# Pairs of (batch, expert) sorted by expert on the chip: 24 of 32 expert units run two batches at a time from stationary weights staged by DMA, 8 one by one

## The reference, cut to what matters

```python
x = x + (einsum('btc,oc->bto', x, W_base) + b_base + 2.0 * lora(x, cond_8))   # first layer
def mlp(x, gate, up, down):                    # 128 -> 512 -> 128
    return (gelu(x @ gate) * (x @ up)) @ down
w, sel = top_k(softmax(cond_8), 2);  w = w / w.sum()
out = sum over the 2 selected experts e of each batch b:  w[b, e] * mlp(x[b], gate[e], up[e], down[e])
out = x + out + mlp(x, shared_gate, shared_up, shared_down)
```

## Time and profile before

| | us |
|---|---|
| median of 3 runs | 146.32 (146.22 to 146.63) |
| the profiled execution: span from first to last instruction | 144.9 |
| TensorE busy | 138.4 |
| VectorE busy | 77.0 |
| ScalarE busy | 73.5 |
| GpSimd busy | 29.7 |
| first product of the shared phase starts | 16.3 |
| first product of the expert phase starts | 52.8 |

### The profile page before, as it was taken

The page is one execution under the profiler, slowest core; times in us unless marked ns, Lnnn a source line. Parts: engine busy times, 40 slices in busy tenths (PEclk is TensorE's granted clock), DMA queues, the critical chain, the costliest instruction groups (busy, mean ns, idle before and its releaser), DMA issues.

```text
span 144.9 us, 3121 instructions
## 1 busy us (share of the span) xinstructions
PE 138.4 (96%) x807; PEld 116.2 (80%) x808; DVE 77.0 (53%) x129; ACT 73.5 (51%) x129; POOL 29.7 (21%) x39
## 2 busy tenths in 40 slices
PE   7899999999899899999999999999999999999991
PEld 6567876767678678889889889889889889889891
DVE  2799899998997986233233233233233233233220
ACT  3235979659759564544344344344344344344340
POOL 2027799831332211011011011011011011010000
PEclk9999999999999999999999999999999999999999
DMA  3997867991000000000000000000000000000001
GB/s 67 286 342 266 295 226 243 264 291 29 0 0 0 0 0 0 5 18 0 18 18 0 18 18 0 18 18 1 18 17 1 18 17 2 18 16 2 18 15 26
DMA packets 10101, 9.44 MB, mean 65 GB/s; under 512 B 1904, under 2 KB 6768, under 8 KB 10096
## 3 DMA queue, kind: packets, MB, share of 16 engines
q1 hardware_dynamic: 9776, 9.31, 21.3%
q10 hardware_dynamic: 320, 0.07, 0.2%
HBM read 8.32 MB, written 1.05 MB: 65 GB/s over the span
## 4 chain that ended last, share of the span: by engine, by line
PE 83%; DVE 5%; ACT 5%; DMA 2%; issue 2%; SPq 0%; DVEq 0%
PE bank L684 20%; PE bank L666 10%; PE bank L668 10%; PE bank L667 10%; PE bank L675 10%; PE bank L623 3%; PE bank L609 3%; PE bank L607 3%; PE bank L608 3%; PE bank L560 3%; DMA xn<-in_x_dram 2%; PE bank L624 2%; PE bank L625 2%; DVE hT_lo L472 2%; PE bank L554 2%
## 5 line engine op out<-in xcount | busy, mean ns | idle before, releaser
L464 DVE SCALAR_TENSOR_TENSOR work<-bank,wgt,work 128x512 f32<-128x512 f32 x32 | 24.0, 751 | 48.1 <-PE bank L668 26.0
L281 ACT ACTIVATE work<-bank 128x512 f32<-128x512 f32 x48 | 28.7, 598 | 39.6 <-PE bank L668 32.0
L684 PE MATMUL bank<-wexd,hT 128*128 x256 | 33.8, 275 | 0.0
L684 PEld LDWEIGHTS bank<-wexd,hT 128*128 128x128 f32 x256 | 31.1, 192 | 0.0
L666 PE MATMUL bank<-wex,xst 128*128 x64 | 27.8, 434 | 0.0
L295 ACT COPY hT<-bank 128x512 f32<-128x512 f32 x32 | 18.8, 586 | 16.6 <-PE bank L675 16.6
L668 PE MATMUL bank<-wex,xst 128*128 x64 | 25.1, 393 | 0.0
L667 PE MATMUL bank<-wex,xst 128*128 x64 | 25.0, 391 | 0.0
L223 POOL CAST xst<-x1s 128x256 fp32r (+1 forms) x16 | 7.3, 462 | 71.1 <-PE bank L668 71.0
L675 PE MATMUL bank<-ident,work 128*128 128x128 f32 x128 | 19.1, 272 | 0.0
L675 PEld LDWEIGHTS bank<-ident,work 128*128 128x128 f32 x128 | 15.8, 139 | 4.1
(11 more groups left out here) (80 smaller groups left out, 135.1 us busy)
## 6 DMA issues: line engine op xcount, KB each, us to landing
raw_ex<-n_L_cond_skill_gate_dram SPq DMA_DIRECT2D x8, 256.0 KB, 3.1
raw_ex<-in_L_cond_skill_up_dram SPq DMA_DIRECT2D x8, 256.0 KB, 4.1
xn<-in_x_dram SPq DMA_DIRECT2D x4, 256.0 KB, 4.2
out_dram<-xT SPq DMA_DIRECT2D x16, 64.0 KB, 1.5
raw_sh<-_L_cond_shared_gate_dram SPq DMA_DIRECT2D x1, 256.0 KB, 4.5
raw_sh<-in_L_cond_shared_up_dram SPq DMA_DIRECT2D x1, 256.0 KB, 5.1
raw_shd<-_L_cond_shared_down_dram SPq DMA_DIRECT2D x1, 256.0 KB, 5.8
b_nat<-in_L_cond_Bs_dram SPq DMA_DIRECT2D x1, 64.0 KB, 2.4
```

What stands on the lines that cost most here:

```text
L281: act.activation(gelu_sb[q], gate_ps[q][:, :], ACT.Gelu_apprx_tanh).then_inc(gelu_done, 1)
L464: dve.scalar_tensor_tensor(h_sb[q], up_ps[q][:, :], wgt[:, k, bass.ds(b, 1)], gelu_sb[q], ALU.mult, ALU.mult).then_inc(h_done, 1)
L684: mm = pe.matmul(bank[4 + j][:, 0:H], hT[:, q, c * P:(c + 1) * P], wexd[:, bass.ds(expert + c * H, H)], start=(k == 0 and c == 0), stop=(k ...
```

## The change

A list of the 32 (batch, expert) entries is built on the chip, sorted by expert. The first 24 places of the list are 12 slots of two entries with the same expert (`NP = 12`); the other 8 places (`LEFT = 24`) are singles. `idx` holds expert offset and batch per place, `wlist` the routing weight.

*The sort.* GpSimd makes more constants and, in steps that wait for each other, the membership of batches in experts, ranks and positions; TensorE does four steps of it (`sort_counts`, `sort_starts`, `sort_singles`, `sort_lists`), VectorE and ScalarE short ones. `sort_lists` stands in TensorE's order after the second unit of shared group 1; the staging of the first singles on GpSimd, and so all of its `ex_ulo` subtractions, stand behind `lists_ready`. The diagonals, `wgt` and `eidx` go.

*The shared phase.* `sum_group` adds into `total` (the tile of x) and the sum transposes and their copies go.

*The expert phase.* Two singles, twelve slots, six singles. Singles run as units did before, from the list, each with a bank of its own and one transposition bank instead of two. In a slot the expert's weights are stationary and the two batches' x is moving, 256 columns at once; the result comes out transposed, so that no transposes are needed, and the down product is made of three fp32r products of 256 columns for each of four chunks. Stationary weights for a slot come from `wst`, three buffers, into which SyncE copies `wex` at the expert's offset from SBUF to SBUF by DMA, 2048 float32 of each of 128 partitions. The split down weights are made per slot, hi by ScalarE (`down_hi`), lo by GpSimd (`down_lo`), and GpSimd stages two batches' x (`stage_slot`). VectorE adds the two halves, with their weights, to `total` (`add_slot`). At the end `merge_transposes` transposes all 16 batches and ScalarE copies them to `base`; results of singles are added; the output leaves in four DMAs of four batches and four single ones.

```diff
@@ SyncE
-            with sp.Fori(0, B) as b:
-                sp.wait_ge(out_ready, b + 1)
-                sp.dma_start(out[bass.ds(b, 1)]..., base[:, bass.ds(b, 1), :]...).then_inc(st_out, 16)
+            sp.wait_ge(lists_ready, 2)
+            sp.wait_ge(ex_hi, 2 * E)
+            sp.wait_ge(ex_glo, E)
+            sp.wait_ge(ex_ulo, E)
+            for p in range(NP):
+                if p >= NBUF:
+                    sp.wait_ge(up_done, PB + 2 * (p - NBUF) + 2)
+                w0 = sp.snap(expert_at(sp, 2 * p) * (GU // DN))
+                sp.dma_start(wst[:, p % NBUF, :].bitcast(F32), wex[:, bass.ds(w0, GU)].bitcast(F32)
+                             ).then_inc(st_w[p % NBUF], 16)
+            sp.wait_ge(res_done, 4)
+            for g in range(NG):
+                sp.dma_start(out[g * GB:(g + 1) * GB].rearrange("b s h -> s b h"),
+                             base[:, g * GB:(g + 1) * GB, :]).then_inc(st_out, 16)
...
@@ GpSimd
+            with pool.Fori(1, NP // NBUF) as i:
+                for j in range(NBUF):
+                    pool.wait_ge(up_done, 2 * NBUF * i + (PB + 2 * j - 2 * NBUF + 2))
+                    stage_slot(NBUF * i + j, j)
+                    down_lo(NBUF * i + (j - 2), (j + 1) % NBUF)
@@ ScalarE
+            def slot(p, j):
+                for n in range(2):
+                    t = 2 * p + (PB + n)
+                    gelu(t, n)
...
+                        split_h_hi(t - 1, 1 - n)
...
+                    if n == 1 and not (isinstance(p, int) and p == NP - 1):
+                        down_hi(p + 1, (j + 1) % NBUF)
@@ VectorE
+            def add_slot(p, j):
+                where = [batch_at(dve, 2 * p + n) for n in range(2)]
+                dve.wait_ge(down_done, 2 * p + (PB + 2))
...
+                for n in range(2):
+                    of_b = total[:, bass.ds(where[n], 1), :].rearrange("p a s -> p (a s)")
+                    dve.scalar_tensor_tensor(of_b, slot_ps[j][:, n * S:(n + 1) * S], wlist[:, bass.ds(2 * p + n, 1)],
+                                             of_b, ALU.mult, ALU.add).then_inc(acc_done, 1)
+            def slot(p, j):
+                for n in range(2):
+                    t = 2 * p + (PB + n)
+                    h_plain(t, n)
+                    if not (isinstance(p, int) and p == 0 and n == 0):
+                        split_h_lo(t - 1, 1 - n, split_count(t - 1))
+                    if n == 1 and not (isinstance(p, int) and p == 0):
+                        add_slot(p - 1, (j + 2) % NBUF)
@@ TensorE
+            def gate_up_slot(j, n):
+                for first, ps, done in ((G_HI, gate_ps[n], gate_done), (U_HI, up_ps[n], up_done)):
+                    for cc in range(2):
+                        c = 2 * n + cc
...
+                        pe.matmul(of_c, w_hi, x_hi, start=True, stop=False)
+                        pe.matmul(of_c, w_hi, x_lo, start=False, stop=False)
+                        mm = pe.matmul(of_c, w_lo, x_hi, start=False, stop=True)
+                    mm.then_inc(done, 1)
+            def slot(p, j, turn):
+                for n in range(2):
+                    if n == 0:
+                        pe.wait_ge(st_w[j], 16 * turn + 16)
+                        pe.wait_ge(xp_ready, 2 * p + 2)
...
+                    gate_up_slot(j, n)
...
+                        down_slot(p - 1, (j + 2) % NBUF, n)
```

More of the change, by code:

```diff
@@ L338, in _ @@
-            with act.Fori(4, NE - 3, 4) as n0:
-                for n in range(4):
-                    gelu(n0 + (NU + n), n % 2)
-                    copy_hT(n0 + (NU + n - 1), (n + 1) % 2)
-            copy_hT(NU + NE - 1, 1)
+            gelu(NU, 0)
+            split_h_hi(NU - 1, 1)
+            act.wait_ge(ld_down, 32)
+            gelu(NU + 1, 1)
+            copy_hT(0)
+            down_hi(0, 0)
+            for p in range(NBUF):
+                slot(p, p)
+            with act.Fori(1, NP // NBUF - 1) as i:
+                for j in range(NBUF):
+                    slot(NBUF * i + j, j)
@@ new lines, in _ @@
+            for p in range(NP - NBUF, NP):
+                slot(p, p % NBUF)
+            gelu(LB, 0)
+            split_h_hi(LB - 1, 1)
+            gelu(LB + 1, 1)
+            copy_hT(NF)
+            gelu(LB + 2, 0)
+            merge(0)
+            copy_hT(NF + 1)
+            merge(1)
+            gelu(LB + 3, 1)
+            merge(2)
+            copy_hT(NF + 2)
+            merge(3)
+            for n in range(4, NL):
+                gelu(LB + n, n % 2)
+                copy_hT(NF + n - 1)
@@ L513, in _ @@
             shared_group(0)
[L514 removed]
+            shared_group(1)
+            with dve.Fori(2, NG) as g:
                 shared_group(g)
[L516 to L525 removed]
@@ L526, in _ @@
[L526 to L534 removed]
+            h_single(0)
+            split_h_lo(NU - 1, 1, NU)
+            h_single(1)
+            sum_group(NG - 1)
+            dve.wait_ge(sum_done, NG)
@@ new lines, in _ @@
+            for p in range(NBUF):
+                slot(p, p)
+            with dve.Fori(1, NP // NBUF) as i:
+                for j in range(NBUF):
+                    slot(NBUF * i + j, j)
+            h_single(NF)
+            split_h_lo(LB - 1, 1, split_count(LB - 1))
+            h_single(NF + 1)
+            add_slot(NP - 1, (NP - 1) % NBUF)
+            h_single(NF + 2)
+            h_single(NF + 3)
+            dve.wait_ge(merged, NG)
+            for s in range(4):
+                result(s)
@@ L536, in _ @@
+            h_single(NF + 4)
+            result(4)
+            h_single(NF + 5)
+            for s in range(5, NF + NL):
+                result(s)
         @block.tensor
@@ L645, in shared_group @@
                     gate_up_shared(g, c)
-                    if c == 1 and first:
-                        pe.wait_ge(setup_sb, 5)
-                        for n in range(2):
-                            expert[n] = expert_of(n)
                     if c >= 2:
@@ L728, in _ @@
-            expert = {n: expert_of(n) for n in (NE - 2, NE - 1)}
-            h_transposes(NE - 1, 1)
-            down_expert(NE - 2, 0, 0, 1, expert[NE - 2])
-            down_expert(NE - 1, 1, 1, 1, expert[NE - 1])
+            gate_up_single(0)
+            down_shared(NG - 1, NC - 2)
+            gate_up_single(1)
+            h_transposes(0)
+            down_shared(NG - 1, NC - 1)
+            pe.wait_ge(ld_down, 32)
+            for p in range(NBUF):
+                slot(p, p, 0)
+            with pe.Fori(1, NP // NBUF) as i:
+                for j in range(NBUF):
+                    slot(NBUF * i + j, j, i)
```

588 lines of the change are left out of this document (409 added, 179 removed).

## The result

Before 146.38 us (median of 4 runs, 146.22 to 146.63), after **149.99 us** (4 runs, 149.44 to 150.38): ratio 1.0245, 95% interval 1.0218 to 1.0272. The changed kernel is slower by 3.6 us. 135.6 us was predicted. Ratios and their intervals go by fast runs, which leaves out every run more than 1.5% above the fastest of its kernel.

A forecast was written before the change was run, and what follows sets the result against it. TensorE was taken as the bound, VectorE busy most of the shared phase. Slots -13.7, first copy +0.8, merge +1.35 and sort +0.8 made -10.75 us, so 146.32 became 135.6 us, range 131 to 145.

The forecast's parts named there:

- Twelve slots (-13.7): Expert phase: twelve paired slots at 4.3 us (ends 4.0 and 5.0) replace 24 units of 2.72, saving 13.7 us.
- rival A: Slots: as forecast, 4.0 to 4.55 us each, total 132.0 to 138.6 us; chance 0.60.
- Register loads "hidden": VectorE's slot additions: batch-number loads taken as hidden under the subtraction before them; 0.6 us if not.
- The first copy's wait (+0.8): Before the first slot: TensorE waits for the first staging copy, +0.8 us (0 to 3).
- the steady state's nothing: Slots: later staging copies, 3.6 us of transfer each, stay below 4.3 and cost nothing.
- Rival C: Slots: SBUF-to-SBUF staging is the bound; at half rate 7.1 us a slot, 169 us total; chance 0.12.
- The merge and the tail (+1.35, 0): Kernel end: 16 final transposes less the last group's give +1.35 us; output stores add 0 (to +1).
- The sort (+0.8; ends to +3.5): Setup and shared group 1: +0.5 us (0 to 1.5) for setup, +0.3 (0 to 2) waiting for the lists.
- 0, with 1 either way: Shared phase: GpSimd's xst casts and ex_ulo subtractions delayed behind the lists cost 0, within 1 us either way.
- B: Slots: VectorE with GpSimd becomes the bound, 4.55 to 5.2 us a slot, total 138.6 to 146.4; chance 0.25.
- D: Slots: TensorE's weight loads no longer hide, 8.1 us a slot, 181 us total; chance 0.03.

The follow-up runs named there:

- neither: On the lists later: constant batch numbers for VectorE's slot additions, and GpSimd's down-weight subtraction only for the first three slots; 142.61 us (one run).
- early loads: On the lists later: register loads outside the slots moved ahead of waits on TensorE, VectorE and SyncE; 142.0 us, ratio to before 0.9681.
- the lists later: On the changed kernel: TensorE's list step, ScalarE's copy of it and VectorE's cast placed two shared units later; 144.93 us, ratio to before 0.9911.
- three-copies kernel: On the lists later: only the first three slots get their weights by a copy, later ones use stale buffers; 145.08 us (one run).
- the spread: On the lists later: GpSimd makes three of eight ex_ulo subtractions around the sort, before it waits for the lists; 148.94 us (median of 4).
- zero products: On the changed kernel: 16 products of zeros, 128 columns each, before TensorE's wait for the lists; 146.87 us, ratio to before 1.0012.

## Why the prediction was wrong

Point by point, in its own steps:

- **Twelve slots (-13.7).** Mis-sized: 54.9 us for 52.3, so the gain was put 2.6 too high. 36 products at 0.120 are 4.32 us, where I had 4.0 to 4.1 from "half of the 512-column start distance". The halving was the fault: it takes some 14 ns that each product costs whatever its width for a cost per column. The 0.2 us that I added for collisions and loads is what they were (0.22, from *neither*). The slot at 4.53 lies still in rival A's range.
- **Register loads "hidden".** In the slots VectorE stands idle for them, but that costs 0.03 us a slot (0.10 once `down_lo` is gone). They cost where I did not count them at all: ahead of `down_single`, of the results, of the last stores. The early loads are 2.9 us faster than the lists later.
- **The first copy's wait (+0.8)** and the steady state's nothing: right. TensorE idles 1.09 us before the first slot. The copies land in 4.6 us (median) with the DMA engines 53% busy, and TensorE has no wait for one in the slots. Rival C fell with it; against it I wrote that the rate of the earlier trace rows is a third above 202 GB/s, but 294 is 1.46 times 202. What the copies do cost is up to 0.09 us a slot by the three-copies kernel, which I had at nothing.
- **The merge and the tail (+1.35, 0).** The register loads again: the results behind the merge come 0.83 apart, `down_single` starts 0.53 to 0.55 late, and with the early loads the last singles take 21.3 us instead of 22.3, so 1.0 of their +2.4; the other 1.4 stays unexplained. SyncE's four loads are the whole of the tail's +2.4: with them early the last stage is 2.6 and 2.7 us, as short as before the change. "0 (to +1)" for the tail was the mistake.
- **The sort (+0.8; ends to +3.5).** The step that failed worst. The chain took 7.2 us, not 3.3: ten steps at 0.39 us where I had eight at 0.3, and six row operations at 0.46 to 1.00 where I had 0.15. The cover was 3.7 us (25.79 to the end of TensorE's second unit), not 4.8, so the wait is 3.51 instead of 0.3. Then a cost came that I had no term for: with 3.5 us of idle time the granted clock fell, which costs 1.6 us in the profiled run and up to 3.1 where it stayed low for longer. The place alone is worth 4.0 us by the profiles and 5.1 by the medians, more than the upper end that I had given the whole sort.
- **The rest of the shared phase.** With the lists placed right it is still 39.0 (or 37.7 in the early loads' profile) against 36.5. One part is the collision at its end and the 1.46 us behind it, shown above. GpSimd's subtractions come in one block behind the sort, and I had called that "0, with 1 either way"; that this block costs the rest is not shown, and moving part of it (the spread) made it worse.

So the sign was lost on two steps, the sort (4.0 to 5.1 of 13.35) and the register loads outside the slots (about 3), and the slots' 2.6 did most of the rest. Without the first of these the change is 0.9% faster than before, without the first two 3.2%. None of my rivals named this: the slots at 4.53 us stayed below the 4.55 where B begins, C and D fell. What stays open: how much of the shared phase's last 1.2 to 2.5 us is GpSimd's late work and how much the chance of the run; the sort's share of the setup, which no run isolates, since the start of the shared phase varies from 16.4 to 18.1 us between profiles of these kernels; the 1.4 us of the last singles; the clock's price of 1.6 us apart from the order of work, since the zero products also shift what VectorE gets to do in the meantime (the further 1.2 to 1.5 us at 6.6 to 6.7 us of low clock come without zero products); and why the clock stayed low for 3.4 us in one profile and twice that in two others.

## What to carry to other kernels

Cost a chain of small dependent steps at the duration of such steps on that engine, and where no row has one, put it where two or three times the estimate is still covered: a wait of 3.5 us on TensorE cost 2.4 here, and the clock that fell behind it 1.6 to 3.1 more. A register load with its arithmetic takes 0.5 to 0.7 us of its engine's queue: count each, put it ahead of a wait and never between a chain's links. When products are made narrower, take the measured pace at both widths as a line with a constant, not as a proportion.

## What the runs showed of the hardware that was not expected

- After 3.5 us of idle time TensorE was granted 0.50 of its clock, for 3.4 us in one profile and for 6.6 to 6.7 in two others with the same wait; products of 512 columns went from 0.228 to 0.43 us apart. Behind 2.79 us of idle time (the spread) it fell as well. With 0.96 us of idle time (the lists later) it stayed at 1.00.
- A one-pass product costs its columns at 2.4 GHz plus 12 to 16 ns: 0.229, 0.175 and 0.119 us at 512, 384 and 256 columns.
- A GpSimd operation on 16 partitions x 32 elements takes 0.46 us, and 1.00 once; on 16 x 1 it is 0.18 to 0.34.
- A VectorE subtraction of 0.68 us lasted 3.82 beside a run of GpSimd instructions. Beside the DMA traffic of the slots alone (some 210 to 220 GB/s, *neither*) it kept its 0.68.
- One value from SBUF to a register costs VectorE's queue 0.30 for the load and one or two steps of arithmetic of up to 0.2, some 0.5 to 0.7 in all.
- SBUF to SBUF, 1 MB lands 4.6 us (median; 4.5 to 6.7) after its issue, no slower than the 4.85 that I had from the rate of the earlier trace rows and a latency.
